# A four-block transformer kernel: row sums on ScalarE, one comparison for whole parts, other first loads, context products ahead, weighing shared out

## What is computed

```python
def _L0_xattn_ref(Q, K, V, ...):          # HD = 8, NH = 16
    q = (Q @ Wq.T + bq).reshape(n, ql, NH, HD)     # k and v alike, from the context
    attn = jnp.einsum('nlhd,nled->nlhe', q, k) / jnp.sqrt(HD)   # heads of one token
    attn = softmax(attn); ctx = jnp.einsum('nlhe,nled->nlhd', attn, v)
    return ctx @ Wo.T + bo
def _L0_ffn_ref(x, W1, b1, W2, b2):       # E = 8 experts, 128 -> 512 -> 128
    h = jnp.mod(x_flat[:, :2].sum(axis=1).astype(jnp.int32), E)
    sel = jnp.stack([h, jnp.mod(h + 1, E)], axis=1)
    ...                                    # half the sum of the two experts
def _L1_xattn_ref(vis, lang, ...):        # over the 64 tokens of a sequence
    attn = softmax((vis@W_vk.T+b_vk) @ (lang@W_lk.T+b_lk).T * C ** -0.5)
    return attn @ (lang@W_lv.T+b_lv) + attn @ (attn.T @ (vis@W_vv.T+b_vv))
def _L1_ffn_ref(x, gate_w, gate_bias, w1, w3, w2, sw1, sw3, sw2):
    # softmax scores, the two best of 8 by score + bias weigh silu(x@w1)*(x@w3)@w2,
    # and a shared expert of twice the width is added to all tokens
x = x + tanh(g_xattn[0]) * _L0_xattn_ref(_layernorm(x), ctx_1024, ctx_1024, ...)
x = x + tanh(g_ffn[0]) * _L0_ffn_ref(_layernorm(x), ...)
x = x + tanh(g_xattn[1]) * _L1_xattn_ref(_layernorm(x), ctx_1024, ...)
x = x + tanh(g_ffn[1]) * _L1_ffn_ref(_layernorm(x), ...)
```

## Time and profile before

| | |
|---|---|
| median of 3 runs | 1307.96 us (1305.18 to 1308.02) |
| the profiled execution | 1305.32 us |
| its span | 1303.6 us |
| busy of the span | PE 85%, DVE 78%, POOL 49%, ACT 45% |
| mean granted TensorE clock | 0.959 |

### The profile page before, as it was taken

One profiled execution on the slowest core, in us unless ns is written; L12 is line 12 of the kernel. 1 busy time (PEld: TensorE's weight loads), 2 busy tenths in 40 slices (PEclk: granted clock), 3 DMA queues, 4 the chain that ended last, 5 costly groups with the idle time before them and its releaser, 6 DMA issues.

```text
span 1303.6 us, 23736 instructions
## 1 busy us (share of the span) xinstructions
PE 1113.0 (85%) x7464; PEld 960.2 (74%) x7464; DVE 1010.9 (78%) x2393; ACT 586.5 (45%) x1506; POOL 637.0 (49%) x377
## 2 busy tenths in 40 slices
PE   5145544899969998799889999999999999999998
PEld 3133333789858988688788888889888888888887
DVE  2999999989999899898537444445688888888887
ACT  2212222465636555355454645454344444444443
POOL 4889997898788987899340110101011111111200
PEclk9999985799989999799899999999999999999999
DMA  6101112889748886589666255552000000000000
GB/s 226 49 25 41 40 41 73 264 269 284 224 151 263 278 253 208 187 240 294 189 198 206 78 176 160 174 162 79 22 25 25 25 25 25 26 25 25 26 9 17
DMA packets 125035, 166.41 MB, mean 128 GB/s; under 512 B 10032, under 2 KB 67568, under 8 KB 124912
## 3 DMA queue, kind: packets, MB, share of 16 engines
q1 hardware_dynamic: 119792, 152.31, 38.1%
q0 software_dynamic: 5120, 12.59, 2.9%
HBM read 137.60 MB, written 27.26 MB: 126 GB/s over the span
## 4 chain that ended last, share of the span: by engine, by line
PE 56%; DVE 25%; issue 8%; POOL 7%; ACT 2%; DMA 1%; SPq 0%; DVEq 0%; POOLq 0%; ACTq 0%
PE ZB L1276 8%; DVE q_sb L898 6%; PE YB L1290 6%; PE YD L1328 5%; DVE s L873 4%; PE ZD L1244 4%; PE ZD L1246 4%; PE ZD L1245 4%; POOL prod L586 3%; PE YB L1328 3%; PE ZB L1244 2%; DVE own_prod L862 2%; PE ZB L1246 2%; PE ZB L1245 2%; POOL xs L596 2%
## 5 line engine op out<-in xcount | busy, mean ns | idle before, releaser
L562 POOL TENSOR_TENSOR rstd<-ve,neghalf 128x4 f32<-128x4 f32 x64 | 65.6, 1025 | 516.6 <-DVE ve L827 515.2
L683 ACT ACTIVATE hid<-ZB,w2b 128x128 f32<-128x128 f32 x768 | 215.8, 378 | 159.0 <-PE YB L1290 78.5
L574 POOL TENSOR_TENSOR prod<-q_sb,kv_sb 128x2048 f32<-128x2048 f32 x48 | 216.3, 4507 | 51.9 <-DVE q_sb L898 31.6
L586 POOL TENSOR_TENSOR prod<-s,kv_sb 128x2048 f32<-128x2048 f32 x48 | 215.2, 4505 | 10.6 <-DVE q_sb L898 10.5
L1276 PE MATMUL ZB<-bt,w1b 128*128 128x128 f32 x1536 | 213.2, 284 | 4.9 <-ACT hid L683 4.7
L1276 PEld LDWEIGHTS ZB<-bt,w1b 128*128 128x128 f32 x1536 | 197.0, 200 | 8.5 <-issue 8.0
L1290 PE MATMUL YB<-w2b,hid 128*128 128x128 f32 x1024 | 141.4, 282 | 0.0
L1290 PEld LDWEIGHTS YB<-w2b,hid 128*128 128x128 f32 x1024 | 129.1, 194 | 14.2 <-ACT hid L683 8.0
L705 ACT ACTIVATE own_prod<-ZD 128x512 f32<-128x512 f32 x102 | 61.1, 599 | 154.6 <-PE ZD L1246 152.3
L1095 DVE TENSOR_TENSOR prod<-own_prod,ZD 128x512 f32<-128x512 f32 x102 | 69.5, 682 | 75.0 <-ACT own_prod L705 51.7
L1110 DVE SCALAR_TENSOR_TENSOR own_prod<-YD,gate,own_prod 128x128 f32<-128x128 f32 x320 | 89.7, 342 | 46.5 <-PE YD L1328 44.6
(11 more groups left out here) (249 smaller groups left out, 2321.0 us busy)
## 6 DMA issues: line engine op xcount, KB each, us to landing
w2b<-in_w SPq DMA_DIRECT2D x96, 516.0 KB
w1b<-in_w SPq DMA_DIRECT2D x96, 512.0 KB
xb<-xs SPq DMA_DIRECT2D x96, 128.0 KB
ctx_t<-in_ctx SPq DMA_DIRECT2D x32, 256.0 KB
x2d<-x2s SPq DMA_DIRECT2D x48, 128.0 KB
x<-in_x SPq DMA_DIRECT2D x16, 256.0 KB
xs<-zrow SPq DMA_DIRECT2D x4, 1024.0 KB, 10.5
xrow<-in_x SPq DMA_DIRECT2D x16, 256.0 KB, 3.6
```

Source lines behind the costliest of these rows:

```text
L574: pool.tensor_tensor(out=prod[:, t % 2, :].rearrange("p (h e d) -> p h e d", h=HEADS, e=HEADS), in0=q.unsqueeze(2).broadcast_to([P, HEADS, ...
L586: pool.tensor_tensor(out=prod[:, (t + 1) % 2, :].rearrange("p (h d e) -> p h d e", h=HEADS, e=HEADS), in0=s0[:, t, :, :].unsqueeze(2).broa ...
L683: act.activation(hid[n % 2][:, j, k * RT:(k + 1) * RT], ZB[j // 2][:, at:at + RT], ACT.Relu, bias=w2b[t % 3][:, k, e, FJ * D + j:FJ * D + ...
```

## The change

- **First norm's sums.** For chunks 1 to 15 ACT takes them: `sums_of_rows` (four ACTIVATE Copy with an accumulator output, k = 12) and `sums_of_squares` (four Square, k = 0), both writing a spill tile. DVE keeps two small operations, `means_of_rows` (k = 14) and `variances_of_rows` (k = 2). Chunk 0 keeps `norm_stats`.
- **One comparison.** In `pick_group` two comparisons of 68 elements and a subtraction become one comparison of 136, and `modv` is shifted.
- **First loads.** x and a row of biases come first, the small weights in two parts, and PE waits at the start only for the first part and for `bias_lo`. Chunk 0 has an order of its own (`kv0`, `xt0`, `q`, `kv1`), later constants are made at half 16, PE waits for the rest at half 24, and the zero fill of `xs` (four DMAs of 1 MB) goes from the front to halves 24 to 36.
- **Context products.** `lk` and the context part of `val` are computed for all chunks at halves 31 to 91 (`languages`), ACT evacuates them, SP stores them to memory and loads them again in `cross`. `val` then adds the loaded tile instead of a bias row.
- **Weighing.** For chunks 5 to 15 the routed units 2 to 5 are weighed by ACT (`unit_weighed`, four ACTIVATE Copy with a pointer scale) and added to `xd` by POOL (`add_unit`); the other sums stay on DVE, from unit 6 on one half later.

```diff
+LANG_AT = [16 * (c // 4) + 31 + (0, 2, 9, 12)[c % 4] for c in range(NC)]
+FIRST_ACT = next(d for d in range(NC) if 2 * C0[d] + 16 > EXPERTS_END + 4)
+BY_ACT = (2, 3, 4, 5)
-C_FIRST = {0: "lk", 1: "vk", 2: "vv", 4: "bdt"}
+C_FIRST = {1: "vk", 2: "vv", 4: "bdt"}
...
+    if s == -1:
+        return {3: [(1, "kv0", 0)], 5: [(0, "xt0", 0)], 7: [(0, "q", 0)], 8: [(1, "kv1", 0)]}.get(k, [])
...
+            def add_unit(d, u):
+                n = WEIGHED[d, u]
+                if u == BY_ACT[0]:
+                    pool.wait_ge(xd_s.sem, STEP[d, 1])
+                else:
+                    pool.wait_ge(added.sem, n - 1)
+                pool.wait_ge(y_s.sem, n)
+                pool.tensor_tensor(out=xd[:], in0=xd[:], in1=y_act[n % 2][:], op=ALU.add).then_inc(added.sem, 1)
...
+            def sums_of_rows(c):
+                if has(c - 1):
+                    act.wait_ge(ln_stats[0].sem, ln_stats[0].at(c - 1))
+                act.wait_ge(ld_x.sem, ld_x.at(c))
+                for j in range(TILES):
+                    last = act.activation(spill[:, j, :], x0[:, j, :], ACT.Copy, accum_out=sums0[:, 0, j:j + 1])
+                last.then_inc(sums0_s.sem, 1)
+
+            def sums_of_squares(c):
+                act.wait_ge(ln_stats[0].sem, ln_stats[0].at(c, 1))
+                for j in range(TILES):
+                    last = act.activation(spill[:, j, :], x0[:, j, :], ACT.Square, bias=nmean[:, 0, j:j + 1], accum_out=sums0[:, 1, j:j + 1])
+                last.then_inc(sums0_s.sem, 1)
...
+            def unit_weighed(d, u):
+                n = WEIGHED[d, u]
+                if n > 2:
+                    act.wait_ge(added.sem, n - 2)
+                act.wait_ge(route.sem, route.at(d))
+                act.wait_ge(pe_f.sem, pe_f.at(d, u))
+                b = unit_sums[SUM[d, u][0]]
+                for j in range(TILES):
+                    last = act.activation(y_act[n % 2][:, j, :], b[:, j * P:(j + 1) * P], ACT.Copy, scale=gate[:, j, u - SHARED:u - SHARED + 1])
+                last.then_inc(y_s.sem, 1)
...
+            def means_of_rows(c):
+                dve.wait_ge(sums0_s.sem, sums0_s.at(c - 1, 1))
+                dve.wait_ge(ln_rstd[0].sem, ln_rstd[0].at(c - 1))
+                dve.tensor_scalar(nmean[:, 0, :], sums0[:, 0, :], -1.0 / D, None, ALU.mult).then_inc(ln_stats[0].sem, 1)
+
+            def variances_of_rows(c):
+                dve.wait_ge(sums0_s.sem, sums0_s.at(c - 1))
+                dve.tensor_scalar(ve[:, 0, :], sums0[:, 1, :], 1.0 / D, EPS, ALU.mult, ALU.add).then_inc(ln_stats[0].sem, 2)
...
-                dve.tensor_tensor(out=hge[:], in0=hs, in1=th_, op=ALU.is_ge).then_inc(s, 1)
-                dve.scalar_tensor_tensor(out=hle, in0=hs, scalar=-1.0, in1=th_, op0=ALU.mult, op1=ALU.is_ge).then_inc(s, 1)
-                dve.wait_ge(pick.sem, pick.at(r, 3))
-                dve.tensor_tensor(out=hge[:], in0=hge[:], in1=hle, op=ALU.subtract).then_inc(s, 1)
+                dve.tensor_tensor(out=hge[:], in0=hs, in1=th_, op=ALU.is_gt).then_inc(s, 1)
...
+            def languages(c):
+                if has(c - 1):
+                    pe.wait_ge(lang_s.sem, lang_s.at(c - 1))
+                else:
+                    pe.wait_ge(raw_lo.sem, raw_lo.at(PIECES - 1))
+                pe.wait_ge(ld_cl[c % 2].sem, ld_cl[c % 2].at(c // 2))
+                pe.matmul(ZB[0][:], ws[:, WLK:WLK + P], ctx_l[c % 2], start=True, stop=True).then_inc(pe_lang.sem, 1)
+                bias_rows_of(ZB[1][:, :], BLV, D, TILES)
+                by_token(ZB[1], ctx_l[c % 2], WLV, D, start=False).then_inc(pe_lang.sem, 1)
...
-                        pe.matmul(b[:, js], ctx2_t[:, js], ws[:, WLV:WLV + D], start=True, stop=False)
-                        last = pe.matmul(b[:, js], blockdiag[:, j, :], vv_sb[:, j, :], start=False, stop=True)
+                        last = pe.matmul(b[:, js], blockdiag[:, j, :], vv_sb[:, j, :], start=True, stop=True)
...
-            pe.wait_ge(s_rows, 16)
-            pe.wait_ge(s_dve0, DVE_CONSTS)
-            pe.wait_ge(s_w2u, 16)
+            pe.wait_ge(s_dve0, 1)
```

More of the change, by code:

```diff
@@ L82 @@
 XB = 4
+LANG_AT = [16 * (c // 4) + 31 + (0, 2, 9, 12)[c % 4] for c in range(NC)]
+LANG = {half: c for c, half in enumerate(LANG_AT)}
 UNIT_IN = {1: 0, 2: 1, 4: 2, 5: 3, 7: 4, 8: 5, 10: 6, 11: 7, 13: 8, 14: 9}
 UNIT_OUT = {pos + 3: u for pos, u in UNIT_IN.items()}
-C_FIRST = {0: "lk", 1: "vk", 2: "vv", 4: "bdt"}
+FIRST_ACT = next(d for d in range(NC) if 2 * C0[d] + 16 > EXPERTS_END + 4)
+BY_ACT = (2, 3, 4, 5)
+WEIGHED = {(d, u): (d - FIRST_ACT) * len(BY_ACT) + i + 1 for d in range(FIRST_ACT, NC) for i, u in enumerate(BY_ACT)}
+STEP = {}
+for _d in range(NC):
+    for _u in range(1, UNITS):
+        if (_d, _u) not in WEIGHED:
+            STEP[_d, _u] = len(STEP) + 1
+C_FIRST = {1: "vk", 2: "vv", 4: "bdt"}
 C_LATER = {0: "xt2", 1: "sc", 4: "val", 5: "att", 7: "xt3"}
@@ L101, in d_parts @@
 def d_parts(tick):
-    return [(c, tick - C0[c] - 8) for c in range(NC) if 0 <= tick - C0[c] - 8 <= 8]
+    return [(c, tick - C0[c] - 8) for c in range(NC) if 0 <= tick - C0[c] - 8 <= 9]
 def has(c):
@@ L469, in _ @@
                 p, a, r = s + 1, s, s - 1
-                if k == 7 and has(p + 1):
+                if k == (7 if p > 0 else 10) and has(p + 1):
                     filled(sp, "kv1", p)
@@ L509, in _ @@
                         load_pair(t + XB)
+                for c in range(NC):
+                    if half == (LANG_AT[c - 2] + 1 if has(c - 2) else LANG_AT[c] - 4):
+                        if has(c - 2):
+                            sp.wait_ge(pe_lang.sem, pe_lang.at(c - 2))
+                        sp.dma_start(ctx_l[c % 2], ctx_in[:, c * CH:(c + 1) * CH]).then_inc(ld_cl[c % 2].sem, 16)
+                if half - 2 in LANG:
+                    c = LANG[half - 2]
+                    sp.wait_ge(lang_s.sem, lang_s.at(c))
+                    sp.dma_start(lk_d[c], lang_k[c % 2]).then_inc(st_lang[c % 2].sem, 16)
+                    sp.dma_start(lv_d[c], lang_v[c % 2]).then_inc(st_lang[c % 2].sem, 16)
                 if not later:
@@ L637, in _ @@
                             gather(c, (2, 3))
+                for d, kd in d_parts(tick):
+                    u = UNIT_OUT.get(2 * kd + later - 1)
+                    if (d, u) in WEIGHED:
+                        add_unit(d, u)
         @block.scalar
@@ L723, in _ @@
                     plain(ot[:], "ot", r)
+                if half == 4:
+                    normed(0, lambda j: xn0[:, j, :], lambda j: x0[:, j, :], 0)
                 if k == 5 and has(p):
                     keys_values(p, 0)
-                if k in (5, 6) and has(p):
+                if k in (5, 6) and has(p) and p > 0:
                     normed(0, lambda j: xn0[:, j, :], lambda j: x0[:, j, :], p, (0, 1) if k == 5 else (2, 3))
@@ L729, in _ @@
                     exp_heads(a, 0)
-                if k == 7 and has(p):
+                if k == (7 if p > 0 else 9) and has(p):
                     keys_values(p, 1)
-                if k == 8 and has(p):
+                if half == 14:
+                    weights()
+                if k == (8 if p > 0 else 6) and has(p):
                     plain(xt0[:], "xt0", p)
@@ L1125, in _ @@
                 row = xrow[r % 2]
+                if half == 16:
+                    later_consts()
                 if k == 0 and has(r):
@@ L1162, in _ @@
                     own_times_v(a)
+                if k == 14 and has(p + 1):
+                    means_of_rows(p + 1)
                 if k == 15:
```

179 lines of the change are left out of this document (119 added, 60 removed).

## The result

The changed kernel takes **1337.89 us** (median of four runs, 1337.18 to 1340.4), the kernel before 1306.92 in the same comparison: the ratio is 1.0242, with a 95% interval of 1.0222 to 1.0261. It is slower by 2.4%, where 1278 was forecast. The profiled execution has a span of 1335.8 us.

What follows compares the result with a forecast made beforehand. It took GpSimd to bound the first attention and TensorE the stages with experts and the last. 6.5 + 2.3 + 5.2 + 14.2 = 28.2 us off 1305.3 gave 1277.1, put at 1278; range 1271 to 1286, eight in ten 1258 to 1295.

Steps and rivals of the forecast that it cites:

- The first attention: Attention chunks: VectorE loses some 1.5 us each, but GpSimd's list limits the gain to 0.57 in four chunks, 2.3 us.
- The sums on ScalarE hold up the relus: Rival, slower side: in 10 attention chunks with experts, ScalarE's sums delay relus; 1312, or 1344 at twice the price; chance 0.08.
- The start: Start of the kernel: TensorE begins 3.0 us earlier and kv1 behind q saves 3.5; 6.5 us, bounds 3.5 to 10.
- `lk` and `val` beside the experts: Second attention with experts, TensorE full: both products come off, lk 6 x 0.86 = 5.2 us, val 0.89 a chunk.
- `val` in the last stage: Last stage, TensorE: the removed half of val saves 0.89 us a chunk, period 32.34 to 31.45; 14.2 over all 16 chunks.
- the weighing: Last stage: moving weighing from VectorE to ScalarE and GpSimd pays nothing and fits by 0.2 to 0.5 us: 0.
- `lk` there at 0, and the wait for `xn` growing: Last stage: removing lk gains 0, at most 8.6 us; TensorE's idle time before xt2 grows from 0.56 to 1.42 us.
- The sum itself: Whole kernel: 28.2 us off 1305.3 makes 1277.1; with the median 2.6 above the profiled execution, forecast put at 1278.
- GpSimd late in the last stage: Rival, last stage: GpSimd's weighing additions delay gather and norm, TensorE waits about 1.1 us a chunk; 1289, chance 0.17.

Runs made afterwards that it cites:

- e1: The changed kernel with its two small first-norm operations on VectorE given a second operand of 128x4 in PSUM: 1292.2 us, ratio 0.9907.
- e2: The changed kernel with the first norm's sums back on VectorE from the second chunk on, all else kept: 1289.0 us, ratio 0.9875.
- e7: e2 with VectorE's six conversions of the index constants moved early, right behind bias_lo: 1284.6 us, ratio 0.9831.
- e12: e2 with lk and val computed in every chunk again, the weighing left on ScalarE and GpSimd: 1301.0 us, ratio 0.9954.
- e5: e2 with the weighing of all units on VectorE again: 1292.0 us, ratio 0.9889.
- e6: e2 with xn of the next chunk ahead of ut_hi on ScalarE: 1282.9 us, ratio 0.9821.
- e8: e5 and e6 together, all weighing on VectorE and xn first on ScalarE: 1287.6 us, ratio 0.9856.
- e9: e7 with xn ahead of ut_hi on ScalarE, only once the experts are done: 1281.0 us, ratio 0.9805.
- e11: e9 with the first norm's sums on ScalarE and the small operations' second operand in PSUM, as e1: 1284.5 us, runs 1276.4 to 1292.9.

## Why the prediction was wrong

The step that failed is the first sentence of **The first attention**: "From VectorE go 1.56 us a chunk of the first norm, against two small operations of 0.15 each". The rows it names are operations that read PSUM; the new ones go from SBUF to SBUF. They measured 3.54 and 1.88 us in the mean, 5.4 us a chunk against 0.3. The trace of before could have warned of it, for it has such an operation, in the source view:

```profile
L922 DVE COPY oh_all<-base x4: 155/257/2229, 84.4 to 542.3; 128x8 f32<-128x8 f32 x4
```

Eight elements a partition, from 155 to 2229 ns: a spread by a factor of 14 that needs a cause. GpSimd's rows give it: the two short ones start while it has no product, and the other two (229.93 + 2.23 and 386.26 + 0.36) end as a product ends, at 232.12 and 386.57. I bounded the new work on ScalarE from both sides and that on VectorE not at all, since "small" seemed to settle it.

The rival for the slower side, "The sums on ScalarE hold up the relus", reached 1312 to 1344 and held the right time by the wrong road. The squares (L730) did wait 58.4 us, but for VectorE's late `nmean` (25.3 us in e1, where it is not held); in e1, with the same sums on ScalarE, the kernel is at 1292. The eight ACTIVATEs cost about what was forecast. Each is followed by a read of the accumulator (ScalarE's groups after):

```profile
L730 ACT ACTIVATE x<-x,nmean 128x128 f32<-128x128 f32 x60 | 23.3, 394 | 58.4 <-DVE nmean L947 58.4
L724 ACT ACTIVATE x<-x 128x128 f32<-128x128 f32 x60 | 17.7, 302 | 7.3 <-DMA x<-in_x 7.3
L724 ACT ACTIVATION_READ_ACCUMULATOR x<-x 128x1 f32 x60 | 11.6, 194 | 0.0
```

With as much again for reading L730's sums (192 ns) that is 64.1 us for 15 chunks, 4.3 each (3.3 forecast, 6.6 the upper end).

The other terms, by e2 against before:

- *The start*, -6.5 forecast. GpSimd's first product came 10.2 us sooner in the changed kernel, the upper bound, and 8.7 in e2. The conversions beside that product took up to 5 us of it back, so that the first `own_prod` came 4.6 us sooner in e2; in e7, which has them early, 8.6.
- *The first attention*, -2.3 from four chunks before the experts. With all of the new norm and no held operation (e1) the first four chunks, from the first `own_prod` to the fifth, take 136.9 us, 138.9 before: 1.9, nearly as forecast. There GpSimd's value products are 34.51 us apart at 104.64 us, the predicted 34.5. The eleven chunks after them take 1.7 us longer in e1 than before, so the stage gives 0.3 in all (one profiled execution of each). In e2, with the old norm, it gives nothing: 4.6 us of lead in the first chunk and in the sixteenth. Another 2.2 us come between there and the first `ut_hi` (665.8 in e2, 672.7 before).
- *`lk` and `val` beside the experts*: from the first `ut_hi` to the sixth, 276.0 us before, 270.1 in e2, 276.7 in e12. The 6.5 us between e2 and e12 stand for five chunks at 1.75, 8.7: three quarters.
- *`val` in the last stage*, 0.89 a chunk: **0** by itself (e5), and the weighing, put at 0, is 0 by itself too (e12). Together they give 0.61 (e2). The sum treated them as separate terms; they are stretches of one loop in which TensorE, VectorE and ScalarE take turns. The removed half was also a little smaller than half: `val` took 1.79 us before and 1.03 in e2 (1082.71 to 1083.74), 0.76 less.
- *`lk` there at 0, and the wait for `xn` growing*: right in the place. TensorE waits 0.8 to 1.1 us for it (1.42 forecast), and the order of `ut_hi` and `xn` on ScalarE is a cause, as e6 shows with 0.4 us and e8 with 0.7.
- *The sum itself*: 1277.1 and the 2.6 us of the median above the profiled execution make 1279.7, where I put 1278: 1.7 us of a miss of 60.
- *GpSimd late in the last stage* was not the right rival in the changed kernel, but it sets the next limit: `xn` waits for `nmr` in e6.

Without the sums on ScalarE the change would have come to 1289, eleven above the forecast, outside its own range of 1271 to 1286 and inside that of eight in ten, 1258 to 1295.

## What to carry to other kernels

Price a small VectorE operation by where its operands lie, not by its size: a TENSOR_SCALAR, COPY or CAST with its source and target both in SBUF can wait out a whole GpSimd instruction, here 4.5 us, so give such operations an end in PSUM or a place where GpSimd is idle. A second operand in PSUM does as well; the one operation with two inputs in SBUF that stood beside a product (`wg_parts` in e7, e9 and e11) was held too. In a trace, compare the end of such an operation with the end of GpSimd's instruction beside it. Before work is taken off an engine, look at what the hand-over puts back on it, and take a wide min/max of an operation of fixed size in the old trace as a question that must be answered. Savings in one loop of engines may be worth nothing apart and something together, so try them in pairs before dropping either.

## What the runs showed of the hardware

The granted clock of TensorE and the time went apart. From 120 to 200 us it reads 0.63 in e2 and 0.87 in e12, the kernel without the context products there, both means over a stretch with both levels, 1.2 and 2.4 GHz; yet the same matmul is not slower in e2 (TensorE's groups in that window, e2 and then e12):

```profile
L1372 PE MATMUL MC<-ws,ctx_t 128*128 128x256 f32 x16 | 6.4, 540 | 0.0
```

```profile
L1365 PE MATMUL MC<-ws,ctx_t 128*128 128x256 f32 x16 | 8.3, 674 | 0.0
```

e2 had TensorE busy 60.6 of these 80 us, e12 32.9. Where TensorE is busy 98.7 of 100 us and the clock reads 1.00 (400 to 500 us in e2), the same matmul takes 405 ns. So a high entry in a stretch where the engine is often idle did not mean fast matmuls; why, no run here shows. The products laid there were free: the first `ut_hi` is at 665.8 in e2 and at 666.1 in e12.
